# Where an expert's small jobs stand between the attention scores: two TensorE items, one GpSimd job and one VectorE reciprocal moved by a place

## The reference, cut to what matters

```
att = softmax(q @ k.T / 8);  out = (att @ v) @ Wo.T + bo
h = silu(xb @ w_gate[e]) * (xb @ w_up[e]);  y[e] = h @ w_down[e]
result = x + out + scatter_add(weight * y) + shared(xn)
```

## Time and profile before

| | before |
|---|---|
| median of 3 runs | 3520.38 us |
| the profiled execution | 3520.27 us |
| its span | 3518.5 us |
| mean granted TensorE clock | 0.989 of full speed |
| busy: TensorE, GpSimd, VectorE, ScalarE | 98%, 78%, 70%, 47% |

### The profile page before, as it was taken

One profiled execution on the slowest core, in us unless ns is written; L12 is line 12 of the kernel. 1 busy time (PEld: TensorE's weight loads), 2 busy tenths in 40 slices (PEclk: granted clock), 3 DMA queues, 4 the chain that ended last, 5 costly groups with the idle time before them and its releaser, 6 DMA issues. The chain is left out here.

```text
span 3518.5 us, 60443 instructions
## 1 busy us (share of the span) xinstructions
PE 3434.4 (98%) x16288; PEld 2081.8 (59%) x16288; DVE 2453.4 (70%) x3127; ACT 1636.5 (47%) x3058; POOL 2733.3 (78%) x2339
## 2 busy tenths in 40 slices
PE   8999799999999999999999999999999999999699
PEld 6888555555555555555555555555555555555487
DVE  7888577777777777777777777777777777776344
ACT  4555344444444444444444444444444444444343
POOL 2111289999999999999999999999999999999421
PEclk9999899999999999999999999999999999999899
DMA  7777856777766767676777777777777777773486
GB/s 241 240 225 216 222 120 164 188 186 185 185 184 185 185 186 185 185 184 182 185 189 189 189 186 189 186 184 184 185 185 185 187 187 184 186 184 96 167 308 227
DMA packets 424397, 669.17 MB, mean 190 GB/s; under 512 B 63456, under 2 KB 229024, under 8 KB 424352
## 3 DMA queue, kind: packets, MB, share of 16 engines
q1 hardware_dynamic: 401568, 637.14, 65.8%
q0 software_dynamic: 14336, 23.08, 3.2%
q10 hardware_dynamic: 8448, 8.39, 0.7%
HBM read 306.91 MB, written 126.12 MB: 123 GB/s over the span
## 5 line engine op out<-in xcount | busy, mean ns | idle before, releaser
L1124 DVE TENSOR_REDUCE merged<-psum 128x1 fp32r<-128x1024 f32 x1024 | 1206.2, 1220 | 629.2 <-PE psum L860 621.4
L1087 ACT ACTIVATE probs<-psum 128x512 f32<-128x512 f32 x2048 | 1078.0, 603 | 1211.1 <-PE psum L835 1209.1
L1311 POOL TENSOR_TENSOR sums<-sums,probs 128x512 f32<-128x512 f32 x768 | 1002.0, 1305 | 60.7 <-ACT probs L1087 1.6
L1312 POOL TENSOR_TENSOR sums<-sums,probs 128x512 f32<-128x512 f32 x768 | 983.1, 1280 | 0.0
L875 PE MATMUL psum<-probs,v_sb 128*64 128x512 f32 x4096 | 936.0, 599 | 0.0
L832 PE MATMUL psum<-q_full,k_full 128*128 128x512 f32 x2048 | 862.4, 421 | 2.5 <-DVE merged L1124 1.6
L835 PE MATMUL psum<-q_rest,k_rest 65*128 65x512 f32 x2048 | 812.1, 397 | 3.0 <-DMA q_rest<-turned 3.0
L875 PEld LDWEIGHTS psum<-probs,v_sb 128*64 128x64 f32 x4096 | 271.4, 136 | 563.6 <-issue 486.5
L832 PEld LDWEIGHTS psum<-q_full,k_full 128*128 128x128 f32 x2048 | 388.6, 190 | 176.1 <-issue 75.8
L835 PEld LDWEIGHTS psum<-q_rest,k_rest 65*128 65x128 f32 x2048 | 390.3, 191 | 72.8 <-DMA q_rest<-turned 3.3
L932 PE MATMUL psum<-x_t,w_qk 128*128 128x512 f32 x1536 | 406.9, 401 | 11.3 <-PEq L1728 6.3
(11 more groups left out here) (150 smaller groups left out, 3052.3 us busy)
## 6 DMA issues: line engine op xcount, KB each, us to landing
x_t<-xt SPq DMA_DIRECT2D x118, 1024.0 KB, 7.3
k_full<-high SPq DMA_DIRECT2D x256, 256.0 KB, 5.3
v<-values SPq DMA_DIRECT2D x64, 512.0 KB, 3.4
w_qk<-wqk_parts SPq DMA_DIRECT2D x64, 512.0 KB
v_sb<-v SPq DMA_DIRECT2D x64, 512.0 KB, 5.5
q_full<-high SPq DMA_DIRECT2D x128, 256.0 KB, 5.8
q_full<-low SPq DMA_DIRECT2D x128, 256.0 KB, 5.8
k_rest<-low SPq DMA_DIRECT2D x128, 256.0 KB, 5.5
```

What stands on the lines that cost most here:

```text
L1087: nc.scalar.activation(probs[:, kt, h, :], score_bank(j), ACT.Exp, scale=SCALE).then_inc(probs_ready, 1)
L1124: nc.vector.tensor_reduce(out=merged[:, q // GROUP, col:col + 1], in_=work[:, 2 * h:2 * h + 2, :].rearrange("p b c -> p (b c)"), axis=AX, ...
L1311: nc.gpsimd.tensor_tensor(total[:, 0, :], first[:, 0, :], probs[:, kt, 0, :], ALU.add)
L1312: nc.gpsimd.tensor_tensor(total[:, 1, :], first[:, 1, :], probs[:, kt, 1, :], ALU.add).then_inc(sums_added, 1)
```

## The change

Four places change. The item XT follows the fifth score of slot 0 instead of the sixth, on TensorE and ScalarE both. The item DN follows the fifth score of slot 3 instead of the sixth, again on both. In slot 2 VectorE does SILU1 behind `low_part` instead of ahead of it. And GpSimd does the gating in front of the addition kt = 3 of the second half instead of kt = 4. No operation is added, removed or resized.

```diff
-ITEMS = ({2: "PJ", 5: "XT"}, {2: "PJ", 4: "GU"}, {2: "PJ"}, {2: "PJ", 5: "DN"})
+ITEMS = ({2: "PJ", 4: "XT"}, {2: "PJ", 4: "GU"}, {2: "PJ"}, {2: "PJ", 4: "DN"})
...
 FILLERS = (((), (), ("RECIP0", "RECIP1")),
            (("RECIP2", "RECIP3"), ("RAW1",), ("TOKEN0", "TOKEN1", "TOKEN2")),
-           (("NORM0", "SILU0", "SILU1"), ("SILU2",), ("NORM1",)),
+           (("NORM0", "SILU0"), ("SILU1", "SILU2"), ("NORM1",)),
            ((), ("RAW0",), ()))
...
                 for kt in range(1, KT):
-                    if (half, kt) == (1, GROUP):
+                    if (half, kt) == (1, GROUP - 1):
                         pool.wait_ge(silu_vec, 3 * s + 3)
```

## The result

The changed kernel takes 3506.62 us (median of 6 runs, 3505.02 to 3508.74) against 3520.35 for the kernel before (6 runs, 3516.8 to 3524.3): a ratio of 0.9962, 95% interval 0.9952 to 0.9973. By the medians that is 13.7 us less, and the interval is some 9.5 to 17. The forecast was 3507. The profiled execution took 3505.8 us with a span of 3504.1, against 3520.27 and 3518.5 before.

The account below looks back on a forecast made before the run. The prediction took TensorE, busy for 98% of the span, to pace the attention stage. Slot 2, slot 0 with the written-out steps, and step 0 summed -9.2 - 4.65 + 0.47 = -13.4 us: forecast 3507, range 3504 to 3513.

Parts of the forecast that it names:

- Slot 2, 9.2 us: TensorE's gap before slot 2's quad, released by the low part, falls from 0.479 to 0.32 in 58 steps: 9.2 us gained.
- Slot 0, 3.8 us in the loop: With XT earlier, slot 0's gap before the quad falls from 0.386 to 0.32: 3.8 us; 4.65 with steps 1, 2, 61.
- Step 0, +0.47: XT in step 0 still waits for its token rows, with two score matmuls left: 0.47 us lost once.
- DN and the gating, 0: Slot 3's quad has no excess, so moving DN wins 0; the earlier gating keeps its inputs ready, reserve 2.7.
- The last steps, 0: TensorE's shorter stall for `hidden` is waited off at GpSimd's sums: 0, upper bound 2.6 us.
- The sum, -13.4: Whole kernel: -9.2 - 4.65 + 0.47 = -13.4 us, from 3520.3 to 3506.9; forecast 3507, chance 0.70.
- TOKEN0, 1.06, with 0.17 left: With GpSimd's phase 0.22 later, TOKEN0 takes about 1.06 instead of 0.84; the reduce behind keeps 0.17 of 0.39.
- Rival (a): TOKEN0 misses its gap, waits one more GpSimd operation, and the reduce is 0.90 late each step: 3559; chance 0.04.
- (b): Slot 0's 0.06 in the loop is TensorE's own issue time, so only 0.85 is gained there: 3510.7; chance 0.12.
- (c): Slot 2's quad isn't released by the low part, leaving -4.65 + 0.47: 3516.1; chance 0.06.
- (e): The tail counts: the last steps give 2.6 us more, 3504.3; chance 0.04.
- (d): In the loop another wait takes over each time, so the order edits shift nothing: about 3520; chance 0.04.

Follow-up runs that it names:

- e1: Kernel before with only SILU1 moved behind the low part in slot 2: 3508.98 us, ratio 0.9974 to the kernel before.
- e2: Kernel before with only XT one place forward in slot 0: 3517.18 us, ratio 0.9995 to the kernel before.
- e3: Kernel before with only DN one place forward and the gating one addition forward: 3520.70 us, ratio 1.0002 to the kernel before.
- e8: Changed kernel with DN and the gating left at their old places (SILU1 and XT alone): 3506.76 us, ratio 0.9968 to the kernel before.
- e5: Changed kernel with GpSimd's gating back at its old place, DN still forward: 3519.52 us, ratio 1.0004 to the kernel before.
- e7: e4 with the last two steps' gating and the last half's row-sum additions moved from GpSimd to VectorE: 3486.71 us, ratio 0.9915 to the kernel before.
- e6: Changed kernel with one spare 0.41 us product at the head of each GpSimd step: 3504.25 us, ratio 0.9967 to the kernel before.
- e4: Changed kernel with the wait for VectorE's reduce put last of the three ahead of each projection (PJ): 3500.61 us, ratio 0.9946 to the kernel before.

## Why the prediction was right, point by point

- **Slot 2, 9.2 us.** Right in mechanism and size: slot 2's gap is 0.320 in all kernels with this edit, 0.159 to 0.160 a step (e1: 8.15 us by steps 3 to 61, within the spread).
- **Slot 0, 3.8 us in the loop.** Right in mechanism, the gap is at the floor. The size is shown less well: 0.065 in slot 0 of the changed kernel and 0.050 in e2, whose period gained half of the forecast. The choice of 4.65 over 0.85, from `x_et` ending 0.10 ahead of the quad although no releaser was named, was the right one. The written-out steps: gap 0.33 instead of 0.59 to 0.61.
- **Step 0, +0.47.** Right within what can be told (0.55, of which up to 0.3 may be the clock). The idle time shown, 0.69, is less than the 0.8 to 0.9 that was forecast; the loss isn't all in that figure.
- **DN and the gating, 0.** Right for the pair (e3, e8). What the prediction treated as a by-product, "the reserve grows to 2.7" (2.5 in the changed kernel, 1524.19 to 1526.71), is what the part lives on: it gave 0.2 for DN's move alone, and e5 shows that the move alone costs 0.18 a step. The working left out its own first term: GpSimd is timed by an exponential ahead of slot 2's quad, DN stands behind that quad, and the quad comes 0.16 sooner. So 0.19 - 0.16 = 0.03 of reserve was left, and e5 shows 0.04: `hidden` at 1534.93, the place of DN at 1534.74 + 0.23 = 1534.97. That is less than the 0.15 that pass from `hidden` to DN's start, which the working also left out. DN then starts 0.11 late, and its second half another 0.07.
- **The last steps, 0.** Right: 126.46 and 126.73. Of the stall in step 63 the prediction said it would shrink; it did not (4.14). It looked at step 63 alone, but it was the stall of step 62 (2.02) that went, and it came back in front of the row sums. The 0 holds for the reason that the prediction gives, GpSimd's unbroken row of work, and e7 bears that out: with work taken from GpSimd the last steps are 10 us shorter.
- **The sum, -13.4.** Steps 3 to 61 gave 12.55 of 13.25 and everything else that the change does near zero; the head's 1.9 in the profiled run is of neither kernel's making. The median's 13.7 and the interval of 9.5 to 17 hold it. That the forecast lies within 0.4 us of the median is finer than the runs can tell.
- **TOKEN0, 1.06, with 0.17 left.** Mis-sized: 1.15 and 0.09. The step that failed is "GpSimd's queue has the same work in sum": it has, but not the same time, as the gating product now runs into NORM1 (0.73 to 1.18).
- **Rival (a), 3559.** Its price was wrong. It let the reduce be late by one more whole addition, 0.90, as if TOKEN0's wait grew with the phase without end. e6 moved the phase by 0.32 more and TOKEN0 fell to 0.28. With one addition as the top, the most it could be is about 1.28, 0.13 longer than now and 0.04 past its reserve of 0.09. e4 and e7 stand there (1.26 to 1.31), and their periods are the shortest of all. The 0.04 of chance was small enough to do no harm.
- **Rivals (b), (c), (e)** fall by e2, e1 and e3, and (d) by the period, 44.511 instead of 44.721.

Open: why e2's period gained 0.031 where its slot gained 0.050 (the spread allows both), and whether e6's 0.027 a step against the changed kernel is the easier TOKEN0 or spread.

## What to carry to other kernels

Compare the same passage in all slots of a step: the shortest is the floor, and what exceeds it is to be had if the last releaser ends just ahead, even where the profile names none. Move a consumer together with its producer's producer: alone, a move that looks free by 0.2 us can cost most of the gain, when another part of the same change brings the consumer forward as well. Put the wait that ends last at the end of a row of waits, since the fulfilled ones behind it are paid on the path; and where a stall is released by an engine that never waits, look at that engine's work: moving the waits about gave nothing here (e3), taking work from it gave 10 us (e7).

## What the hardware showed that I had not expected

- Two fulfilled waits behind one that is released late cost TensorE some 0.15 us each time (e4: the weight load 0.17 sooner after the reduce's start, slot 0 shorter by 0.149).
- Delaying the engine that competes for the ports can shorten the other's work: TOKEN0 0.28 instead of 1.15 us with GpSimd 0.32 us later (e6).
- TensorE can be slower after it has stood still: DN's first two matmuls take 1.19 us behind the stall of 4.14 in the changed kernel, 0.59 in e7 at the same place without a stall. Not every stall does it: behind the wait of 1.49 in step 63 the row sums take 1.07, as in e7 without a stall, though behind the 1.40 of e7's step 62 DN's first two take 1.14. The stretch around DN in step 63 of the changed kernel, and then 50 us of the last two steps, in the changed kernel and in e7 (stretch, its length, busy us of PE, PEld, DVE, ACT, POOL with their instructions, granted clock, DMA share, GB/s):

```profile
3255.00:3261.00 6.00, 4.74 (x12) 3.38 (x14) 0.00 (x0) 1.77 (x4) 5.78 (x7) 0.50 0.00 0
```
```profile
3220.00:3270.00 50.00, 39.90 (x172) 20.44 (x172) 13.57 (x15) 18.88 (x38) 47.60 (x40) 0.92 0.10 24
```
```profile
3210.00:3260.00 50.00, 43.37 (x204) 20.95 (x202) 28.80 (x31) 20.18 (x41) 28.39 (x21) 0.97 0.17 38
```

Behind the stall the granted clock is 0.50 of full speed, the lower level of 1.2 GHz instead of 2.4, which goes with twice the duration. Over 50 us it is 0.92 on average with the stalls and 0.97 without the long ones: such a stall costs its length and a little more behind it. GpSimd is full in the changed kernel (47.60 of 50 us) and not in e7 (28.39), which is what e7 changed.
